# A chunked delta-rule scan in which batch 1 runs two steps behind batch 0 and w @ S is written one quarter on

## The chip, the cores and the metric

One core of a Trainium2 chip. The metric is the device time of one execution in microseconds (us), the median of the runs.

## The reference, cut to what matters

The model takes x of 2 x 1024 x 128 and applies three layers, each on a layer norm of x and added to x: a mixture of experts (top 1 of 8), an attention layer, and the same mixture of experts again. The change lies in the attention layer, in its delta rule, with 4 heads of 32 channels and chunks of 32 tokens, so 32 steps for each of the 2 batches:

```python
def step(S, inp):
    qi, ki, ui, wi = inp
    attn = jnp.tril(qi @ ki.transpose(0, 1, 3, 2))
    u_i = ui - wi @ S
    o_i = qi @ S + attn @ u_i
    return (S + ki.transpose(0, 1, 3, 2) @ u_i, o_i)
S0 = jnp.zeros((b, h, dk, dv), dtype=q.dtype)
S, o = jax.lax.scan(step, S0, (mov(q), mov(k), mov(u), mov(w)))
```

Each step needs the state S that the step before it left. The two batches have states of their own and don't depend on each other.

## The kernel before, in words

The program is a row of blocks that run one after the other: constants, `moe_ffn` (first), `attn_project`, `attn_delta`, `attn_mix`, `moe_ffn` (second). All data are fp32. Within a block each engine has its own program, written out in order, and semaphores join them.

`attn_delta` does in turn: the inverse of each chunk's triangular matrix (16 steps of products by `product`, L760, with masks by VectorE), scores and the u and w of all chunks (`scores`, `product`, `u0`), then the scan (299.56 to 362.05 us of the span), and last `intra`/`add_intra`, the products with u that need no state.

The scan is what the change touches. The state of a batch lies in `SB[:, b, :]`, 128 x 128, four heads as four blocks on the diagonal. For a step n and a batch b the chunk is quarter `c = n % 4` of tile `n // 4`. One step of one batch is a ring of four pieces:

- `w_state` (L886, TensorE): w @ S into partitions 32c to 32c+31 of bank b. The stationary operand is 128 rows x 32 columns, so the product uses all rows of the array and one quarter of its columns, the quarter in which its output lies. It waits for `s_ready`, the state after step n-1.
- `subtract` (L1090, VectorE): u = u - w @ S, on 32 partitions, from bank b into `U` (its tile has the name XN in the profile). It waits for `ws_psum`.
- `add_state` (L901, TensorE): k.T @ u, added into bank 2 + b. Its operands lie on 32 partitions (rows of quarter c), its output on all 128. It waits for `u_ready`.
- `state` (L1095, VectorE): the bank times a block mask, into `SB[:, b, :]` (d_SB). It waits for `s_psum`, and lets `w_state` of the next step go.

Beside the ring stands `q_state` (L893, TensorE): q @ S into the output bank (4 to 7), in quarter c too. It needs the state alone and nothing in the scan waits for it. In the profile every matmul of fp32 shows as two passes, each with its own weight load, so one product is x2, and the two products of both batches x4.

TensorE's program of one step is: w of batch 0, w of batch 1, q of batch 0, q of batch 1, add of batch 0, add of batch 1; in the first eight steps two transposes follow (`turn_fl`, L910, 128 x 128), which have nothing to do with the scan. VectorE's is: subtract 0, subtract 1, state 0, state 1; after steps 7, 15, 23 and 31 two reductions follow (`v_stats`, L1100 and L1101), which have nothing to do with the scan either. Both engines take their instructions in this order. All four w and q products of a step lie in the same column quarter c, and both adds on the same row quarter c.

Of the kernel before, what the change touches and what calls it, by code (L numbers as in the profile page):

```python
# [11 lines left out]
P = 128  # L12
# [664 lines left out]
def attn_delta(nc, cst, mem, banks, B, L, NH):  # L677
# [24 lines left out]
    with ExitStack() as ctx:  # L702
# [28 lines left out]
        m_psum, m_ready = sem("m_psum"), sem("m_ready")  # L731
        ws_psum = sem("ws_psum")
        u_ready = sem("u_ready")
        s_psum, s_ready = sem("s_psum"), sem("s_ready")
        oi_psum, oi_taken = sem("oi_psum"), sem("oi_taken")
# [20 lines left out]
        def product(pe, bank, lhs, slot):  # L756

            for t in range(TB):
                for a in range(NH):
                    mm = pe.matmul(bank[a * C:(a + 1) * C, t * P:(t + 1) * P], lhs(t, a), BD[:, slot, t * NH + a, :], start=True, stop=True)  # L760
            return mm

        def o_place(tile):
# [3 lines left out]
        with nc.Block() as block:  # L767

            @block.tensor
            def _(pe):  # L770
# [109 lines left out]
                def w_state(b, n):  # L880

                    c, t = n % CT, n // CT
                    cols = slice((b * TH + t) * P + c * C, (b * TH + t) * P + (c + 1) * C)
                    if n > 0:
                        pe.wait_ge(s_ready, n * B + b - B + 1)
                    pe.matmul(banks[b][c * C:(c + 1) * C, 0:P], WT[:, cols], SB[:, b, :], start=True, stop=True).then_inc(ws_psum, 1)  # L886

# [8 lines left out]
                def add_state(b, n):  # L896

                    c, t = n % CT, n // CT
                    rows, tile = slice(c * C, (c + 1) * C), b * TH + t
                    pe.wait_ge(u_ready, n * B + b + 1)  # L900
                    pe.matmul(banks[2 + b][:, 0:P], K[rows, tile, :], U[rows, tile, :], start=(n == 0),  # L901
                              stop=(n == STEPS_S - 1), skip_group_check=True).then_inc(s_psum, 1)

# [9 lines left out]

                for n in range(STEPS_S):
                    w_state(0, n)
                    w_state(1, n)
                    if n == STEPS_S // 2:

                        pe.wait_ge(fl_taken, NG)
                    q_state(0, n)  # L920
                    q_state(1, n)
                    add_state(0, n)
                    add_state(1, n)
                    if 2 * n < NT:
                        turn_fl(2 * n)
                        turn_fl(2 * n + 1)

                pe.wait_ge(u_ready, B * STEPS_S)
                pe.wait_ge(s_ready, B * STEPS_S)

# [96 lines left out]
            def _(ve):  # L1027
# [57 lines left out]
                def subtract(b, n):  # L1085

                    c, tile = n % CT, b * TH + n // CT
                    rows = slice(c * C, (c + 1) * C)
                    ve.wait_ge(ws_psum, n * B + b + 1)
                    ve.tensor_tensor(U[rows, tile, :], U[rows, tile, :], banks[b][rows, 0:P], ALU.subtract).then_inc(u_ready, 1)  # L1090

                def state(b, n):

                    ve.wait_ge(s_psum, n * B + b + 1)
                    ve.tensor_tensor(SB[:, b, :], banks[2 + b][:, 0:P], cst["blk"][:], ALU.mult).then_inc(s_ready, 1)  # L1095

# [5 lines left out]

                for n in range(STEPS_S):
                    subtract(0, n)
                    subtract(1, n)
                    state(0, n)
                    state(1, n)
                    if n % 8 == 7:
                        if n == 7:
                            ve.wait_ge(vsq_ready, 1)  # L1110
                        v_stats(n // 8)
# [702 lines left out]
```

## Time and profile before

| | us |
|---|---|
| median of 3 runs | 565.75 |
| the three runs | 565.56, 565.75, 574.91 |
| the profiled execution, its own time | 564.4 |
| its span | 562.6 |
| TensorE busy (share of the span) | 406.0 (72%) |
| VectorE busy (share) | 319.2 (57%) |
| granted TensorE clock, mean over the span | 0.867 |
| the scan, within the span | 299.56 to 362.05 |

The span is the time from the first to the last instruction in the profile; 1.8 us of the execution lie outside of it. PE is a matmul on TensorE, PEld its weight load, DVE is VectorE, ACT ScalarE. A clock of 1.00 is 2.4 GHz, of 0.50 is 1.2 GHz.

### The profile page before, as it was taken

Reading aid. Unit: us, or ns where it says so; the run is one execution under the profiler, and the core shown is the slowest. Engines: PE = TensorE matmul, PEld = TensorE weight load, DVE = VectorE, ACT = ScalarE, POOL = GpSimd, SP = SyncE. Lnnn points to the kernel's source line nnn. Section 1 sums busy time; section 2 is a strip of 40 time slices with the busy share of each in tenths; the row PEclk is TensorE's granted clock in tenths of the full one; section 3 lists DMA queues with packets and bytes.
Section 4 is the critical chain, followed back from the end, with each engine's and each line's share of the span. In section 5 each row is a group of like instructions: output and inputs, shape, how many; then the busy total and the mean of one; then the engine's idle time right before and its main releaser. Section 6 shows DMA issues by size and latency. Waiting matters only on the chain. (4 is left out here: it accounts for less than half of the span.)

```text
span 562.6 us, 12845 instructions
## 1 busy us (share of the span) xinstructions
PE 406.0 (72%) x5009; PEld 319.8 (57%) x5010; DVE 319.2 (57%) x819; ACT 225.3 (40%) x453; POOL 142.4 (25%) x154
## 2 busy tenths in 40 slices
PE   0776599925985668889999988977996370059990
PEld 0664399913545557767787666753454360059980
DVE  4550465436968498777455556455488846026533
ACT  1233055614556367877342000174566221015550
POOL 4427135520006792000000000020222202714441
PEclk9999899976899759999899999986998555569996
DMA  9963401130000000000000000047000082141005
GB/s 190 279 197 91 121 21 38 33 93 2 0 0 1 3 3 4 5 5 3 2 3 1 1 1 1 1 92 152 1 1 0 0 269 81 52 118 36 33 28 164
DMA packets 32709, 29.92 MB, mean 53 GB/s; under 512 B 6800, under 2 KB 25776, under 8 KB 32656
## 3 DMA queue, kind: packets, MB, share of 16 engines
q1 hardware_dynamic: 23760, 20.96, 13.3%
q10 hardware_dynamic: 6400, 3.08, 3.3%
q0 software_dynamic: 2496, 5.13, 2.8%
q8 instruction: 38, 0.62, 0.5%
q14 instruction: 15, 0.12, 0.1%
HBM read 16.54 MB, written 9.21 MB: 46 GB/s over the span
## 5 line engine op out<-in xcount | busy, mean ns | idle before, releaser
L303 ACT ACTIVATE hT<-bank,b1s 128x128 f32<-128x128 f32 x184 | 52.4, 370 | 92.2 <-PE bank L260 91.3
L206 POOL DMA_INDIRECT ysort<-Y,row x46 | 44.8, 974 | 71.3 <-DVE Y L382 65.2
L260 PE MATMUL bank<-xT,w1s 128*128 (+1 forms) x368 | 51.0, 283 | 3.5 <-DVE xT L405 3.5
L276 PE MATMUL bank<-W,hT 128*128 x368 | 50.4, 280 | 3.1 <-ACT hT L303 2.9
L260 PEld LDWEIGHTS bank<-xT,w1s 128*128 128x128 f32 x368 | 46.6, 198 | 4.7 <-DVE xT L405 4.1
L276 PEld LDWEIGHTS bank<-W,hT 128*128 128x128 f32 x368 | 44.6, 191 | 5.3 <-issue 4.8
L1382 POOL TENSOR_TENSOR m_DSQ<-DEL 128x512 f32<-128x512 f32 x4 | 4.1, 1041 | 159.2 <-POOLq L767 156.5
L1054 DVE TENSOR_TENSOR d_BD<-bank,quarter 128x2048 f32<-128x2048 f32 x16 | 36.5, 2288 | 13.5 <-PE bank L760 13.5
L199 POOL DMA_INDIRECT xsort<-xr,pos x32 | 31.4, 980 | 48.4 <-DVE pos L361 39.3
L964 ACT ACTIVATE d_BD<-d_TP 32x512 f32<-32x512 f32 x64 | 40.5, 633 | 0.9
L248 PE MATMUL bank<-ident,xs 128*128 128x128 f32 x46 | 8.3, 318 | 29.3 <-DMA xs<-xsort 29.3
L1095 DVE TENSOR_TENSOR d_SB<-bank,blk 128x128 f32<-128x128 f32 x64 | 16.5, 292 | 17.5 <-PE bank L901 17.5
L760 PE MATMUL bank<-d_BD,d_ATP 128*32 128x128 f32 x512 | 19.5, 293 | 6.4 <-ACT d_BD L964 6.4
L901 PE MATMUL bank<-XN,K 32*128 32x128 f32 x128 | 22.6, 296 | 1.4 <-DVE XN L1090 1.4
L886 PE MATMUL bank<-d_SB,KBT 128*32 128x128 f32 x128 | 20.1, 280 | 4.6 <-DVE d_SB L1095 3.7
L382 DVE TENSOR_TENSOR Y<-bank,b2t 128x128 f32 (+1 forms) x46 | 13.3, 288 | 17.8 <-PE bank L276 14.7
L248 PEld LDWEIGHTS bank<-ident,xs 128*128 128x128 f32 x46 | 6.4, 164 | 29.8 <-issue 29.5
L376 DVE COPY b1s<-b1T 128x4 f32 x46 | 9.2, 200 | 24.5 <-ACT hT L303 10.6
L1000 ACT ACTIVATE d_TMP<-bank 128x512 f32<-128x512 f32 x4 | 2.4, 598 | 48.3 <-PE bank L935 48.3
L1090 DVE TENSOR_TENSOR XN<-XN,bank 32x128 f32<-32x128 f32 x64 | 16.0, 283 | 9.2 <-PE bank L886 9.2
L901 PEld LDWEIGHTS bank<-XN,K 32*128 32x128 f32 x128 | 16.5, 185 | 8.0 <-DVE XN L1090 8.0
L378 DVE COPY w1s<-W 128x512 f32 x46 | 20.8, 453 | 0.0
(297 smaller groups left out, 928.7 us busy)
## 6 DMA issues: line engine op xcount, KB each, us to landing
W<-in_L_ffn_w SPq DMA_DIRECT2D x2, 2048.0 KB, 12.7
xsort<-pad ACTq DMA_DIRECT2D x2, 1483.5 KB, 20.4
xs<-xsort SPq DMA_DIRECT2D x10, 258.0 KB, 4.0
G<-ysort SPq DMA_DIRECT2D x8, 256.0 KB, 4.0
b2bc<-in_L_ffn_b SPq DMA_DIRECT2D x2, 512.0 KB, 19.6
m_pairs<-FS SPq DMA_DIRECT2D x4, 256.0 KB, 5.0
m_pairs<-firT SPq DMA_DIRECT2D x4, 256.0 KB, 4.9
m_pairs<-VP SPq DMA_DIRECT2D x4, 256.0 KB, 5.1
```

Of the source, the lines that this page charges most:

```text
L199: gp.indirect_dma_start(xsort, bass.IndirectOffsetOnAxis(pos[:, t:t + 1], 0), xr[:, t, :], None).then_inc(scattered, 16)
L206: gp.indirect_dma_start(ysort, bass.IndirectOffsetOnAxis(row[:, t:t + 1], 0), Y[:, t, :], None).then_inc(y_stored, 16)
L260: mm = pe.matmul(pH[s % 2][:, j * P:(j + 1) * P], w1s[:, s, j * P:(j + 1) * P], xT[:, bass.ds(t, 1), :], start=True, stop=True)
L276: mm = pe.matmul(pY[s % 2][:, 0:D], hT[:, s % 2, j, :], W2[:, bass.ds(e, 1), j, :], start=(j == 0), stop=(j == FC - 1))
L303: act.activation(hT[:, s % 2, j, :], pH[s % 2][:, j * P:(j + 1) * P], ACT.Gelu, bias=b1s[:, s, j:j + 1]).then_inc(h_ready, 1)
L378: ve.tensor_copy(w1s[:, s, :], W1[:, bass.ds(e, 1), :]).then_inc(w1_staged, 1)
L760: mm = pe.matmul(bank[a * C:(a + 1) * C, t * P:(t + 1) * P], lhs(t, a), BD[:, slot, t * NH + a, :], start=True, stop=True)
L886: pe.matmul(banks[b][c * C:(c + 1) * C, 0:P], WT[:, cols], SB[:, b, :], start=True, stop=True).then_inc(ws_psum, 1)
L901: pe.matmul(banks[2 + b][:, 0:P], K[rows, tile, :], U[rows, tile, :], start=(n == 0), stop=(n == STEPS_S - 1), skip_group_check=True).then ...
L964: cp = act.activation(spread_dst(i % 2, a), blocks(TP[a * C:(a + 1) * C, i % NG, :]), ACT.Copy)
L1054: ve.tensor_tensor(BD[:, 2 + i % 2, :, :].rearrange("p s (a n) -> p s a n", n=C), all_blocks(banks[i % 2][:]), mask, ALU.mult).then_inc(z_ ...
L1095: ve.tensor_tensor(SB[:, b, :], banks[2 + b][:, 0:P], cst["blk"][:], ALU.mult).then_inc(s_ready, 1)
```

## The change

Batch 1 runs two steps behind batch 0 (`LAG = 2`): the loops on TensorE and VectorE now have 34 iterations instead of 32, and iteration n does step n of batch 0 and step n - 2 of batch 1. Iterations 0 and 1 have batch 0 alone, iterations 32 and 33 batch 1 alone. The product w @ S of step n is written to column quarter (n + 1) % 4 of its bank (`w_rows`) and read there by `subtract`, whose other operands stay on quarter n % 4. So in iteration n the w products lie in quarters n+1 (batch 0) and n-1 (batch 1), the q products in quarters n and n-2, each modulo 4: four different ones. The adds lie on row quarters n and n-2. The four semaphores of the ring are kept per batch, each wait being for the same event as before. `turn_fl` stays in iterations 0 to 7, `v_stats` behind iterations 7, 15, 23 and 31.

```diff
--- before.py
+++ after.py
@@ -729,9 +729,7 @@
         ut_psum, ut_ready = sem("ut_psum"), sem("ut_ready")
         u0_psum, u0_ready = sem("u0_psum"), sem("u0_ready")
         m_psum, m_ready = sem("m_psum"), sem("m_ready")
-        ws_psum = sem("ws_psum")
-        u_ready = sem("u_ready")
-        s_psum, s_ready = sem("s_psum"), sem("s_ready")
+        ws_psum, u_ready, s_psum, s_ready = ([sem(f"{n}{b}") for b in range(B)] for n in ("ws_psum", "u_ready", "s_psum", "s_ready"))
         oi_psum, oi_taken = sem("oi_psum"), sem("oi_taken")
         o_psum = sem("o_psum")
         short_fir = sem("short_fir")
@@ -759,6 +757,17 @@
                 for a in range(NH):
                     mm = pe.matmul(bank[a * C:(a + 1) * C, t * P:(t + 1) * P], lhs(t, a), BD[:, slot, t * NH + a, :], start=True, stop=True)
             return mm
+
+        LAG = 2
+
+        def w_rows(b, n):
+
+            c = (n + 1) % CT
+            return slice(c * C, (c + 1) * C)
+
+        def active(b, n):
+
+            return 0 <= n - b * LAG < STEPS_S
 
         def o_place(tile):
 
@@ -882,8 +891,8 @@
                     c, t = n % CT, n // CT
                     cols = slice((b * TH + t) * P + c * C, (b * TH + t) * P + (c + 1) * C)
                     if n > 0:
-                        pe.wait_ge(s_ready, n * B + b - B + 1)
-                    pe.matmul(banks[b][c * C:(c + 1) * C, 0:P], WT[:, cols], SB[:, b, :], start=True, stop=True).then_inc(ws_psum, 1)
+                        pe.wait_ge(s_ready[b], n)
+                    pe.matmul(banks[b][w_rows(b, n), 0:P], WT[:, cols], SB[:, b, :], start=True, stop=True).then_inc(ws_psum[b], 1)
 
                 def q_state(b, n):
 
@@ -897,9 +906,9 @@
 
                     c, t = n % CT, n // CT
                     rows, tile = slice(c * C, (c + 1) * C), b * TH + t
-                    pe.wait_ge(u_ready, n * B + b + 1)
+                    pe.wait_ge(u_ready[b], n + 1)
                     pe.matmul(banks[2 + b][:, 0:P], K[rows, tile, :], U[rows, tile, :], start=(n == 0),
-                              stop=(n == STEPS_S - 1), skip_group_check=True).then_inc(s_psum, 1)
+                              stop=(n == STEPS_S - 1), skip_group_check=True).then_inc(s_psum[b], 1)
 
 
                 def turn_fl(n):
@@ -911,22 +920,24 @@
                     if t == TB - 1:
                         tr.then_inc(fl_psum, 1)
 
-                for n in range(STEPS_S):
-                    w_state(0, n)
-                    w_state(1, n)
+                for n in range(STEPS_S + LAG):
+                    both = [b for b in range(B) if active(b, n)]
+                    for b in both:
+                        w_state(b, n - b * LAG)
                     if n == STEPS_S // 2:
 
                         pe.wait_ge(fl_taken, NG)
-                    q_state(0, n)
-                    q_state(1, n)
-                    add_state(0, n)
-                    add_state(1, n)
+                    for b in both:
+                        q_state(b, n - b * LAG)
+                    for b in both:
+                        add_state(b, n - b * LAG)
                     if 2 * n < NT:
                         turn_fl(2 * n)
                         turn_fl(2 * n + 1)
 
-                pe.wait_ge(u_ready, B * STEPS_S)
-                pe.wait_ge(s_ready, B * STEPS_S)
+                for b in range(B):
+                    pe.wait_ge(u_ready[b], STEPS_S)
+                    pe.wait_ge(s_ready[b], STEPS_S)
 
                 def intra(g):
 
@@ -1086,13 +1097,13 @@
 
                     c, tile = n % CT, b * TH + n // CT
                     rows = slice(c * C, (c + 1) * C)
-                    ve.wait_ge(ws_psum, n * B + b + 1)
-                    ve.tensor_tensor(U[rows, tile, :], U[rows, tile, :], banks[b][rows, 0:P], ALU.subtract).then_inc(u_ready, 1)
+                    ve.wait_ge(ws_psum[b], n + 1)
+                    ve.tensor_tensor(U[rows, tile, :], U[rows, tile, :], banks[b][w_rows(b, n), 0:P], ALU.subtract).then_inc(u_ready[b], 1)
 
                 def state(b, n):
 
-                    ve.wait_ge(s_psum, n * B + b + 1)
-                    ve.tensor_tensor(SB[:, b, :], banks[2 + b][:, 0:P], cst["blk"][:], ALU.mult).then_inc(s_ready, 1)
+                    ve.wait_ge(s_psum[b], n + 1)
+                    ve.tensor_tensor(SB[:, b, :], banks[2 + b][:, 0:P], cst["blk"][:], ALU.mult).then_inc(s_ready[b], 1)
 
                 def v_stats(c):
 
@@ -1100,12 +1111,13 @@
                     ve.tensor_reduce(mem["ST"][:, part, 1, 3, :], V[:, part, :].rearrange("p t (h d) -> p t h d", h=NH), AX.X, ALU.max)
                     ve.tensor_reduce(mem["ms"][:, part, 3, :], VSQ[:, part, :].rearrange("p t (h d) -> p t h d", h=NH), AX.X, ALU.add)
 
-                for n in range(STEPS_S):
-                    subtract(0, n)
-                    subtract(1, n)
-                    state(0, n)
-                    state(1, n)
-                    if n % 8 == 7:
+                for n in range(STEPS_S + LAG):
+                    both = [b for b in range(B) if active(b, n)]
+                    for b in both:
+                        subtract(b, n - b * LAG)
+                    for b in both:
+                        state(b, n - b * LAG)
+                    if n % 8 == 7 and n < STEPS_S:
                         if n == 7:
                             ve.wait_ge(vsq_ready, 1)
                         v_stats(n // 8)
```

TensorE at the end of the scan. Banks 0 and 1 take w @ S of batch 0 and 1, banks 5 and 7 q @ S, banks 2 and 3 the state; L935 is `intra`, the stage behind the scan. Before:

```order
L886 MATMUL bank0<-d_SB,KBT 32x128
L886 MATMUL bank1<-d_SB,KBT 32x128
L893 MATMUL bank5<-d_SB,QT 32x128
L893 MATMUL bank7<-d_SB,QT 32x128
L901 MATMUL bank2<-XN,K 128x128
L901 MATMUL bank3<-XN,K 128x128
L935 MATMUL bank0<-d_BD,XN 32x128 x16
```

The same place after the change (w is L895, q L902, add L910, `intra` L946):

```order
L895 MATMUL bank0<-d_SB,KBT 32x128
L895 MATMUL bank1<-d_SB,KBT 32x128
L902 MATMUL bank5<-d_SB,QT 32x128
L902 MATMUL bank7<-d_SB,QT 32x128
L910 MATMUL bank2<-XN,K 128x128
L910 MATMUL bank3<-XN,K 128x128
L895 MATMUL bank1<-d_SB,KBT 32x128
L902 MATMUL bank7<-d_SB,QT 32x128
L910 MATMUL bank3<-XN,K 128x128
L895 MATMUL bank1<-d_SB,KBT 32x128
L902 MATMUL bank7<-d_SB,QT 32x128
L910 MATMUL bank3<-XN,K 128x128
```

The order within an iteration is as it was; what has moved is that two iterations with batch 1 alone stand ahead of `intra` (and two with batch 0 alone at the start of the scan).

VectorE at the same place; L1100 and L1101 are the reductions of `v_stats`, banks as above. Before:

```order
L1090 TENSOR_TENSOR XN<-XN,bank0 32x128
L1090 TENSOR_TENSOR XN<-XN,bank1 32x128
L1095 TENSOR_TENSOR d_SB<-bank2,blk 128x128
L1095 TENSOR_TENSOR d_SB<-bank3,blk 128x128
L1100 TENSOR_REDUCE ST<-V 128x4x4
L1101 TENSOR_REDUCE ms<-d_BD 128x4x4
```

After (subtract is L1101, state L1106, the reductions L1111 and L1112):

```order
L1101 TENSOR_TENSOR XN<-XN,bank0 32x128
L1101 TENSOR_TENSOR XN<-XN,bank1 32x128
L1106 TENSOR_TENSOR d_SB<-bank2,blk 128x128
L1106 TENSOR_TENSOR d_SB<-bank3,blk 128x128
L1111 TENSOR_REDUCE ST<-V 128x4x4
L1112 TENSOR_REDUCE ms<-d_BD 128x4x4
L1101 TENSOR_TENSOR XN<-XN,bank1 32x128
L1106 TENSOR_TENSOR d_SB<-bank3,blk 128x128
L1101 TENSOR_TENSOR XN<-XN,bank1 32x128
L1106 TENSOR_TENSOR d_SB<-bank3,blk 128x128
```

The last pair of reductions, which was the end of VectorE's part of the scan, now stands ahead of the last two steps of batch 1.

## Rows read from the trace of the kernel before

**Rows 1.** Who waited for whom in the scan: total us, times, longest us

```profile
DVE d_SB L1095 <- PE bank L901: 17.5, 32, 0.6
...
PEld bank L886 <- DVE d_SB L1095: 9.4, 31, 0.4
DVE XN L1090 <- PE bank L886: 9.2, 29, 0.6
PEld bank L901 <- DVE XN L1090: 8.0, 32, 0.8
```

**Rows 2.** The scan: length, busy PE, PEld, DVE, ACT, POOL, TensorE's clock, DMA

```profile
299.60:362.05 62.45, 56.99 (x400) 41.59 (x400) 35.85 (x135) 2.98 (x5) 0.00 (x0) 1.00 0.00 1
```

**Rows 3.** Timeline of one ordinary step: start, us, engine, line; idle before it

```profile
333.34 0.36 PEld L886 LDWEIGHTS bank<-d_SB,KBT 128*32 128x32 f32 x4 [0.35 <-DVE d_SB L1095]
333.78 0.50 DVE L1090 TENSOR_TENSOR XN<-XN,bank 32x128 f32<-32x128 f32 x2 [0.27 <-PE bank L886]
333.81 0.60 PE L893 MATMUL bank<-d_SB,QT 128*32 128x128 f32 x4
334.33 0.52 PEld L901 LDWEIGHTS bank<-XN,K 32*128 32x128 f32 x4 [0.20 <-DVE XN L1090]
334.86 0.52 DVE L1095 TENSOR_TENSOR d_SB<-bank,blk 128x128 f32<-128x128 f32 x2 [0.57 <-PE bank L901]
335.20 0.36 PEld L886 LDWEIGHTS bank<-d_SB,KBT 128*32 128x32 f32 x4 [0.35 <-DVE d_SB L1095]
```

**Rows 4.** Single products, passes or VectorE instructions, from narrower windows

```profile
329.82 0.27 PE L893 MATMUL bank<-d_SB,QT 128*32 128x128 f32 x1
...
333.34 0.41 PE L886 MATMUL bank<-d_SB,KBT 128*32 128x128 f32 x2 [0.16 <-DVE d_SB L1095]
...
334.01 0.28 DVE L1090 TENSOR_TENSOR XN<-XN,bank 32x128 f32<-32x128 f32 x1
...
334.34 0.48 PE L901 MATMUL bank<-XN,K 32*128 32x128 f32 x2
...
334.86 0.29 DVE L1095 TENSOR_TENSOR d_SB<-bank,blk 128x128 f32<-128x128 f32 x1 [0.57 <-PE bank L901]
```

**Rows 5.** Timeline of a step with the two transposes

```profile
312.53 0.71 PE L901 MATMUL bank<-XN,K 32*128 32x128 f32 x4
...
313.16 0.20 PEld L910 LDWEIGHTS bank<-ident,FLt 128*128 128x128 f32 x2
...
313.53 0.36 PEld L886 LDWEIGHTS bank<-d_SB,KBT 128*32 128x32 f32 x4 [0.17 <-DVE d_SB L1095]
...
315.53 0.36 PEld L886 LDWEIGHTS bank<-d_SB,KBT 128*32 128x32 f32 x4 [0.17 <-DVE d_SB L1095]
```

**Rows 6.** Timeline of a step behind the two reductions of VectorE

```profile
330.54 0.52 DVE L1095 TENSOR_TENSOR d_SB<-bank,blk 128x128 f32<-128x128 f32 x2 [0.56 <-PE bank L901]
...
330.97 0.68 DVE L1100 TENSOR_REDUCE ST<-V 128x16 f32<-128x512 f32 x1
...
331.56 0.68 DVE L1101 TENSOR_REDUCE ms<-d_BD 128x16 f32<-128x512 f32 x1
332.16 0.46 DVE L1090 TENSOR_TENSOR XN<-XN,bank 32x128 f32<-32x128 f32 x2
```

**Rows 7.** Timeline behind the scan: 16 products of L935, four quarters in turn

```profile
365.16 1.08 PE L935 MATMUL bank<-d_ATP,XN 128*32 128x128 f32 x32
```

**Rows 8.** Busy us by stretch, as rows 2: before and behind the scan

```profile
276.82:280.20 3.38, 3.15 (x41) 2.75 (x33) 1.32 (x3) 2.83 (x5) 0.00 (x0) 1.00 0.00 0
280.23:283.60 3.37, 3.37 (x41) 2.71 (x43) 1.32 (x2) 0.00 (x0) 0.00 (x0) 0.50 0.00 0
...
372.40:375.79 3.39, 1.31 (x8) 0.84 (x8) 3.28 (x7) 1.90 (x5) 1.87 (x2) 1.00 0.51 117
375.80:379.20 3.40, 2.44 (x10) 1.44 (x11) 3.40 (x6) 3.31 (x7) 1.04 (x1) 0.50 0.98 205
```

**Rows 9.** Timeline before the scan, at half clock: 16 products of `product`, four quarters in turn

```profile
273.64 1.93 PE L760 MATMUL bank<-d_BD,VB 128*32 128x128 f32 x32
```

## The prediction

> **What bounds the kernel now.** I read the waits of the scan first, then the scan as one stretch, then one step in narrow windows. In the waits the reader is to see a ring: VectorE waits for TensorE 32 times ahead of the state (17.5 us in all) and 29 times ahead of the subtract (9.2), and TensorE's weight loads wait for VectorE ahead of w (9.4) and of the add (8.0) [rows 1]. No other engine and no DMA is in it; ScalarE is busy 2.98 us of 62.45, and TensorE has its full clock throughout [rows 2].
>
> The narrow windows tell which wait is real. In the ordinary step the w products start at 333.34 and those of the next step at 335.20, so a step takes 1.86 us [rows 3]. Batch 0's ring alone is shorter. The second w pass ends 0.41 after the start of the first [rows 4] and the subtract starts at 333.78, +0.44 [rows 3]; it takes 0.28 [rows 4] and ends at 334.06. The add starts only at 334.33 [rows 3]. The profile puts this wait down to VectorE, but batch 0's subtract had been done for 0.27. Between a VectorE end and the weight load it releases there are otherwise only 0.05 (the state of batch 0 starts at 334.86, takes 0.29, and w loads at 335.20 [rows 3, 4]), so the add could load at 334.11. What holds it is TensorE's own order: the four q passes stand ahead of it, start 0.11 apart from 333.81 (four in 0.60 [rows 3], one takes 0.27 [rows 4]), the last at 334.14, and the load of another shape comes 0.19 to 0.20 behind it [rows 3]. These four passes and the four of w all lie in one column quarter. The two add passes take 0.48 to their end (0.49 from the load), the state starts 0.04 later, takes 0.29 [rows 4], and the release 0.05.
>
> **The change part by part.**
>
> *Quarters.* Of products in four quarters by turns there is a row: 32 passes of L935, the same shape as w and q, take 1.08 us, so (1.08 - 0.27) / 31 = 0.026 per pass against 0.11 in one quarter [rows 7]. With w of batch 1 and both q in three other quarters, the q passes need not queue behind w. Batch 1's state ends 0.22 to 0.29 after batch 0's, so its w loads at about +0.29, the q passes start right behind it, and the last starts at about +0.29 + 0.02 + 0.11 + 0.03 = +0.45; with 0.20 for the change of shape the add could load at +0.65. Batch 0's subtract lets it go at +0.44 + 0.28 + 0.05 = +0.77. So q is off the path, with 0.12 to spare, and the ring sets the step: 0.44 + 0.28 + 0.05 + 0.49 + 0.04 + 0.29 + 0.05 = 1.64 us. An ordinary step saves 0.22. What is late next is VectorE and the latency of each piece, not TensorE's order.
>
> *Batch 1 in the ring.* Its pieces follow batch 0's. Now the second subtract starts 0.22 after the first [rows 3, 4]. No row shows two subtracts on different quarters, so its place is bounded: +0.22 as now, or, with nothing laid over the first and a gap of 0.05, +0.33. I take 0.28, the end of the first. Batch 1's add then loads at 0.77 + 0.28 + 0.01 = +1.06 and ends at +1.55, its state +1.59 to +1.88, its w at +1.93: the offset stays 0.29, the step stays 1.64. The two adds lie on different row quarters and need not queue either; even if they did batch 0's last pass starts at +0.99 and batch 1's first at +1.06, so nothing changes. Reading bank b one quarter off the output costs nothing as an operation added; the nearest durations are 0.28 for the 32-partition subtract and 0.29 for the 128-partition state [rows 4], so the bound is 0 to 0.01 x 34 = 0.3 us, and no reason makes it a gain. I take 0.
>
> By the Trainium skill, VectorE: DVE Perf Modes, section "Two Vector instructions with no wait between them", an instruction that starts on another quadrant than the one before is held until that one has finished. No run here shows it yet; by it the second subtract comes at +0.28 and the result is the one taken above, without it the sum would be 0.4 us lower.
>
> *Steps with transposes.* Before they take 2.00 (313.53 to 315.53 [rows 5]): the transposes load 0.19 after the last add pass starts (312.53 + 0.71 - 0.27 = 312.97), and w 0.37 after that, 0.14 later than its state allows. After: batch 1's last add pass starts at 1.06 + 0.215 = +1.28 (two passes end 0.49 from the load, the last takes 0.27), the transposes load at +1.47, w at +1.84. Iterations 2 to 7 take 1.84; by the two bounds of the second subtract 1.78 or 1.89, so 6 x 0.06 = 0.4 us either way. In iterations 0 and 1 batch 1 is absent, the transposes load at +0.99 + 0.19 = +1.18 and are over at +1.55: hidden, 1.64.
>
> *The reductions.* The first starts 0.20 after batch 1's state starts (330.54 + 0.23 = 330.77, then 330.97), and the subtract comes 1.19 later, 1.39 after that state's start [rows 6]. Before, w behind them starts at 330.54 + 0.29 + 0.05 = 330.88 and the next at 333.34 [rows 3]: a step of 2.46, so 0.60 more than 1.86, three times, while the fourth pair lies behind the scan. In the shorter ring there is less slack: the subtract is due 0.50 after batch 1's state starts (1.64 + 0.44 - 1.59), so it is 0.89 late, behind iterations 15 and 23; 0.69 behind iteration 7, whose w is 0.20 late anyway; and behind iteration 31, where batch 1 alone goes on (due at 0.29 + 0.05 + 0.44 = 0.78), 0.61. Sum 3.1 us. They now start as early as they do now; if the subtract had to await the end of the second reduction (332.24 instead of 332.16), 4 x 0.08 = 0.3 more.
>
> *Lag.* 34 iterations instead of 32, the added two at 1.64. They stand ahead of the stage behind the scan, which needs the last u of batch 1, and nothing hides them: 3.3 us, in the sum below.
>
> *Sum.* 28 x 1.64 + 6 x 1.84 + 3.1 = 45.9 + 11.0 + 3.1 = 60.0 us. Before: 8 x 2.00 + 24 x 1.86 + about 1.6 = 62.2; the trace has 62.49 (299.56 to 362.05). The gain is 62.5 - 60.0 = 2.5. No DMA is issued in the scan and no queue is passed. Taken from the profiled execution's 564.4 that is 562.0; the median of the runs is 1.35 above that execution, so I forecast 563.4.
>
> **The rivals.**
>
> *The clock falls in the scan: slower than before.* The granted clock never fell in the scan, where TensorE was busy 57.0 of 62.45 us [rows 2]. But busy time does not guard it: it was 0.50 in the stretch from 280.23, behind one busy for 3.15 of 3.38 us, and in the stretch from 375.80, behind one busy for 1.31 of 3.39 with eight matmuls [rows 8]. After the change the same products lie upon each other and then pause, longest at the reductions, and at the scan's end batch 1 is alone. At half clock 32 passes take 1.93 instead of 1.08 [rows 7, 9], a pass round 0.11 more; with two rounds and a longer last pass in w and again in the add I estimate 0.5 to 0.6 per step, 2.2 instead of 1.64. So a stretch of 3.4 us at half clock holds 1.5 steps for 2.1 and loses 0.9. It decides once more than about three such stretches fall, which eats the 2.5. If the clock falls at each of the four reductions and once behind the scan (up to 1.5 there), the loss is 5.1 and the time 568.5; if every other stretch of the scan is cold, some nine, it is 8 and the time about 571. Against it speaks that the number of passes per us rises.
>
> *The quarters don't overlap.* Then the q passes follow w of batch 1: they start at +0.52, the last at +0.85, the add loads at +1.05 instead of +0.77, and an ordinary iteration takes 1.92, one with transposes about 2.05. 4 x 1.64 + 6 x 2.05 + 24 x 1.92 + about 2.3 for the reductions = 67.2, 4.7 more than before: 570.5. The row of L935 speaks against it [rows 7]: by it neighbours in other quarters do overlap. The Trainium skill, TensorE: Matmul & The Clock Gate, section "Part 3: Packing small matmuls — row/col tiling", says that "LDWEIGHTS overlaps with in-flight MATMULs only when row_grp differs"; all four products here use all rows, so by that rule this rival would hold. The trace disagrees with it, with 0.026 us per pass.
>
> *The lag and the reductions eat all.* If only the ordinary steps gained and the transposed ones did not (6 x 0.16), with the reductions 0.3 dearer, the gain is 1.2: 564.6. That is inside the forecast's own spread.
>
> **How the numbers follow.** Forecast, ring of 1.64 with the clock held or down once: 0.63. Clock falls repeatedly: 0.26. No overlap: 0.07. Gain larger than 4.5, by a reason that I don't see: 0.04. The forecast's own range is 561.5 to 565.5: the bounds above give 0.4 + 0.3 + 0.3, and a single clock stretch falling elsewhere behind the scan, since all later work starts 2.5 us sooner, some 1.5. The range reaches into the clock rival: 560.8 to 570.0. 2% are 11.3 us, about what a measurement of this kernel can tell from no change; no case of mine gains that, and only a scan cold for most of its length (34 x 0.55 = 19 us) loses it. So faster 0.01, same 0.94, slower 0.05.
>
> **What would show it.** Right: w starts 1.64 apart in ordinary iterations and 1.84 with transposes; the add loads 0.05 behind its own subtract; the q passes start within 0.2 of w of batch 1; the scan lasts 60 us from first w to last state. Wrong: a granted clock under 1.00 in the scan; q passes 0.11 apart behind w of batch 1; a second subtract much later than 0.33 behind the first; a subtract longer than 0.29.

## The result and the profile after

| | before | after |
|---|---|---|
| median of 4 runs each, us | 570.33 | 583.05 |
| all runs | 565.56, 565.75, 574.91, 579.55 | 582.10, 582.83, 583.27, 583.49 |
| ratio, 95% interval | | 1.029 [1.026, 1.033] |
| span of the profiled execution | 562.6 | 580.5 |
| ahead of the scan | 299.6 | 302.1 |
| the scan | 62.5 | 79.0 |
| behind the scan | 200.5 | 199.4 |
| mean granted clock over the span | 0.867 | 0.789 |

The change makes the kernel slower, and the scan alone is 16.5 of the 17.9 us by which the span grew. The ratio leaves out executions that fell in a slower state, so it is not 583.05 / 570.33 = 1.022. Further runs of the unchanged kernel, reported below, spread from 566.8 to 589.5 us, so what is firm of the loss is the part that the profile shows in the scan. The page's clock row (40 slices, here of 14.5 us each) shows where to look:

```profile
PE 424.5 (73%) x5009; PEld 323.6 (56%) x5010; DVE 322.2 (56%) x819; ACT 225.7 (39%) x453; POOL 142.2 (24%) x154
...
PEclk9999799958797679999775555566899555559996
```

Slices 22 to 26 (counted from 1) lie wholly in the scan, and stand at 5, half clock. TensorE's busy time went up by 18.5 us with the same number of matmuls, 12.1 of it in the scan (69.06 against 56.99), where the same matmuls take longer. The busy rows by stretch (length, busy PE, PEld, DVE, ACT, POOL, clock, DMA), first the whole scan as in [rows 2], then its two parts, then a stretch behind it that is at full clock again:

```profile
302.08:381.08 79.00, 69.06 (x400) 38.94 (x400) 41.59 (x136) 2.39 (x4) 0.00 (x0) 0.52 0.00 1
...
301.50:304.80 3.30, 1.91 (x14) 1.01 (x14) 1.38 (x4) 0.49 (x1) 0.00 (x0) 1.00 0.00 0
304.95:381.00 76.05, 67.00 (x387) 37.86 (x386) 40.65 (x133) 2.39 (x4) 0.00 (x0) 0.50 0.00 1
387.00:397.00 10.00, 7.35 (x104) 5.96 (x96) 3.73 (x6) 6.43 (x11) 3.03 (x3) 1.00 0.14 34
```

The scan starts at full clock (2.4 GHz), loses it 2.8 us later, in iteration 1, with batch 0 alone in the ring, and runs at 1.2 GHz to its end. Only the dense stage behind it brings the clock back, at 386.8 (from 381.2 to 386.7 TensorE was busy for 5.47 of 5.50 us). In the 3.30 us ahead of the fall TensorE was busy for 1.91 us with 14 passes. The first 3.30 us of the scan in the kernel before, to be held against that:

```profile
299.60:302.90 3.30, 3.30 (x25) 2.61 (x26) 1.49 (x6) 0.59 (x1) 0.00 (x0) 1.00 0.00 0
```

The waits show the same ring as [rows 1], with the wait ahead of the add now on top:

```profile
PEld bank L910 <- DVE XN L1101: 22.5, 34, 1.3
DVE d_SB L1106 <- PE bank L910: 19.9, 34, 0.9
...
DVE XN L1101 <- PE bank L895: 15.7, 30, 0.9
PEld bank L895 <- DVE d_SB L1106: 10.6, 30, 0.7
```

TensorE's load for the add waits for VectorE 22.5 us instead of 8.0: the q passes no longer stand in its way, it really waits for the subtract (and at half clock most pieces of the ring take longer). One iteration at half clock, to be held against the step of [rows 3] (w is L895, q L902, subtract L1101, add L910, state L1106):

```profile
342.40 0.45 PEld L895 LDWEIGHTS bank<-d_SB,KBT 128*32 128x32 f32 x3 [0.36 <-DVE d_SB L1106]
...
342.73 0.43 PE L902 MATMUL bank<-d_SB,QT 128*32 128x128 f32 x2
...
342.95 0.43 PE L902 MATMUL bank<-d_SB,QT 128*32 128x128 f32 x2
343.08 0.60 DVE L1101 TENSOR_TENSOR XN<-XN,bank 32x128 f32<-32x128 f32 x2 [0.41 <-PE bank L895]
343.42 0.81 PEld L910 LDWEIGHTS bank<-XN,K 32*128 32x128 f32 x4 [0.50 <-DVE XN L1101]
...
344.25 0.61 DVE L1106 TENSOR_TENSOR d_SB<-bank,blk 128x128 f32<-128x128 f32 x2 [0.57 <-PE bank L910]
344.59 0.44 PEld L895 LDWEIGHTS bank<-d_SB,KBT 128*32 128x32 f32 x3 [0.36 <-DVE d_SB L1106]
```

From 342.40 to 344.59 are 2.19 us against 1.86 at full clock before. The order of things is the one aimed at: the four q passes start in two pairs, at 342.73 and 342.95, right behind w of batch 1, and the add loads 0.06 behind the end of its own subtract (343.08 + 0.28). At full clock one iteration was to be seen whole in this run, the first, with batch 0 alone and its two transposes:

```profile
302.08 0.11 PEld L895 LDWEIGHTS bank<-d_SB,KBT 128*32 128x32 f32 x1 [1.19 <-DVE XN L1072]
...
302.59 0.28 DVE L1101 TENSOR_TENSOR XN<-XN,bank 32x128 f32<-32x128 f32 x1 [0.57 <-PE bank L895]
302.92 0.29 PEld L910 LDWEIGHTS bank<-XN,K 32*128 32x128 f32 x2 [0.70 <-DVE XN L1101]
...
303.79 0.11 PEld L895 LDWEIGHTS bank<-d_SB,KBT 128*32 128x32 f32 x1 [0.25 <-DVE d_SB L1106]
```

That is 1.71 us, with the subtract 0.51 behind w instead of the 0.44 of [rows 3].

Not all iterations take 2.19. The six with both batches and transposes take 2.67 each (w at 305.65 and, six later, at 321.64), and the ones behind the second and third pair of reductions 2.97 (339.43 to 342.40):

```profile
305.65 0.14 PEld L895 LDWEIGHTS bank<-d_SB,KBT 128*32 128x32 f32 x2 [0.33 <-DVE d_SB L1106]
...
321.64 0.13 PEld L895 LDWEIGHTS bank<-d_SB,KBT 128*32 128x32 f32 x2 [0.33 <-issue]
...
339.43 0.45 PEld L895 LDWEIGHTS bank<-d_SB,KBT 128*32 128x32 f32 x3 [0.36 <-DVE d_SB L1106]
...
340.21 0.68 DVE L1112 TENSOR_REDUCE ms<-d_BD 128x16 f32<-128x512 f32 x1
340.90 0.60 DVE L1101 TENSOR_TENSOR XN<-XN,bank 32x128 f32<-32x128 f32 x2
```

### The profile page after: what moved, and what is told of

Same layout as the page of the kernel before. It is cut to its first block and busy times, and to the rows that moved or that the text cites. A ratio compares the mean times of both kernels' runs of the same rounds, so it can differ in the third digit from the quotient of the medians.

```text
span 580.5 us, 12846 instructions
## 1 busy us (share of the span) xinstructions
PE 424.5 (73%) x5009; PEld 323.6 (56%) x5010; DVE 322.2 (56%) x819; ACT 225.7 (39%) x453; POOL 142.2 (24%) x154
## 5 line engine op out<-in xcount | busy, mean ns | idle before, releaser
L910 PE MATMUL bank<-XN,K 32*128 32x128 f32 x128 | 35.9, 491 | 7.4 <-DVE XN L1101 6.5
L910 PEld LDWEIGHTS bank<-XN,K 32*128 32x128 f32 x128 | 26.0, 302 | 22.5 <-DVE XN L1101 22.5
L895 PE MATMUL bank<-d_SB,KBT 128*32 128x128 f32 x128 | 28.6, 417 | 3.0 <-DVE XN L1072 0.8
L248 PE MATMUL bank<-ident,xs 128*128 128x128 f32 x46 | 8.8, 328 | 29.3 <-DMA xs<-xsort 29.3
L1106 DVE TENSOR_TENSOR d_SB<-bank,blk 128x128 f32<-128x128 f32 x64 | 18.7, 292 | 20.7 <-PE bank L910 19.9
L1101 DVE TENSOR_TENSOR XN<-XN,bank 32x128 f32<-32x128 f32 x64 | 18.2, 284 | 16.8 <-PE bank L895 15.7
L248 PEld LDWEIGHTS bank<-ident,xs 128*128 128x128 f32 x46 | 6.7, 170 | 30.0 <-issue 29.6
L902 PE MATMUL bank<-d_SB,QT 128*32 128x128 f32 x128 | 21.3, 417 | 0.0
## 6 DMA issues: line engine op xcount, KB each, us to landing
W<-in_L_ffn_w SPq DMA_DIRECT2D x2, 2048.0 KB, 12.1
```

The lines of the kernel that those rows point to most:

```text
L248: tr = pe.transpose(pX[c % 2][:, t * P:(t + 1) * P], xs[:, g + t, 0:D], ident[:])
L895: pe.matmul(banks[b][w_rows(b, n), 0:P], WT[:, cols], SB[:, b, :], start=True, stop=True).then_inc(ws_psum[b], 1)
L902: pe.matmul(o_place(tile)[c * C:(c + 1) * C, :], QT[:, cols], SB[:, b, :], start=(tile % TB == 0), stop=True, skip_group_check=True)
```

## The experiments

The runs were made in several jobs on different chips, each with runs of the kernel before beside it, and times of different jobs are not to be compared (the unchanged kernel's ran from 565.6 to 589.5 us). What is compared is therefore the scan within each profile: its length from first w to last state, its clock, and the time from one w to the next. The clock was looked at in one profiled execution of each run. The rest of the span can't be held against the change: without the run behind a pause, the scans start at 299.6 to 312.4 us, and what follows them takes 199 to 203. A table comes first, the runs one by one behind it.

Four theories of the lost clock go through the expectations: A, TensorE has too little to do in each step; B, the lag is to blame; C, only passes that lie upon each other in several quarters lose the clock; D, the thin entrance loses it, and a scan of this kind stays at the clock with which it enters. An ordinary iteration is one without transposes and not behind reductions.

| run | scan, us | clock in it | ordinary iteration, us | whole run, us (before in the same job) |
|---|---|---|---|---|
| before | 62.5 | 1.00 | 1.86 | 565.56 to 579.55 |
| the change | 79.0 | 0.52 | 2.18 | 583.05 (570.33) |
| lag alone | 82.8 | 0.51 | 2.37 | 590.62 (573.22) |
| quarters alone | 84.9 | 0.51 | 2.60 | 591.18 (573.22) |
| change + one product | 68.3 | 0.85 | 1.65 to 1.76 | 576.69 (573.22) |
| change + two products | 65.6 | 1.00 | 1.85 | 576.20 (573.22) |
| before without q | 68.6 | 0.63 | 1.65, then 2.19 | 581.87 (586.44) |
| before behind a pause | 101.8 | 0.50 | 3.02 | 620.52 (586.44) |
| change + products at the start | 73.8 | 0.62 | 2.18 after the start | 585.53 (586.44) |
| change + products tuned | 72.5 | 0.73 | 1.65 to 1.75, then 2.38 | 584.33 (586.44) |
| before again | 62.5 | 1.00 | 1.86 | 580.15 (571.74) |
| change + two products again | 65.6 | 1.00 | 1.85 | 584.42 (571.74) |
| before + products | 62.8 | 1.00 | 1.86 | 571.82 (571.74) |
| tuned + 32-row products | 62.5 | 1.00 | 1.66 to 1.76 | 564.78 (581.03) |

**The two halves of the change.** Lag alone:

```diff
-            c = (n + 1) % CT
+            c = n % CT
```

> The change without its quarters: batch 1 two steps behind, w @ S in quarter n as before. Then w and q of one batch share a quarter, and the passes lie two by two upon each other instead of four. Theory A (the clock falls because the w and q passes lie upon each other, so that TensorE's array is at work for less of each step): less overlap than in the change, so a clock above the change's; if it holds, a step of 1.70 and 565 us, if it falls nonetheless, 2.2 to 2.3 per step and 583. Theory B (the lag alone is to blame: adds on two row quarters, thin first iterations): the clock falls as in the change, 583 us.

Quarters alone:

```diff
-        LAG = 2
+        LAG = 0
```

> The change without its lag: 32 iterations with both batches at the same step, w @ S one quarter on. Both w in one quarter, both q in the next. Theory A: overlap two by two as in the run with the lag alone, and the same fate as that run (clock held: 1.65 to 1.7 per step, 557 to 560 us; fallen: 2.2 per step, 578). Theory B: the clock holds, since nothing is staggered, 557 to 560 us.

Both lose the clock. The scan of the lag alone, then of the quarters alone:

```profile
305.36:388.15 82.79, 74.71 (x400) 47.13 (x400) 39.29 (x136) 2.57 (x5) 0.00 (x0) 0.51 0.00 1
```

```profile
301.36:386.25 84.89, 83.30 (x400) 52.98 (x400) 40.02 (x135) 2.56 (x5) 0.00 (x0) 0.51 0.00 1
```

So theory B falls: with nothing staggered the clock goes too. Theory A had said that both share one fate, and they do; its other guess for the lag alone, a clock above the change's, was wrong. Each half takes q passes off TensorE's order by laying them on w passes, and either is enough. In a kernel at half clock the two still add up in the way intended (quarters alone 2.60, lag alone 2.37, both 2.18; before 3.02, by a run below): the less stands in TensorE's order, the shorter the step. TensorE is busy 83.3 of 84.9 us in the second row, and has half the clock: the busy column says nothing on whether the clock is held.

**More work in the scan.** Products of constants were added to the change between the q products and the adds, in the quarter of the last q product so that they follow it; nobody reads them. With one:

```diff
+        FILL = lambda n: 4 if n % 8 == 0 and n > 0 else 1
...
+                    for k in range(FILL(n)):
+                        q4 = slice((n + 2) % CT * C, ((n + 2) % CT + 1) * C)
+                        pe.matmul(banks[2][q4, P:2 * P], cst["ones"][:, 0:C], cst["blk"][:], start=False, stop=True, skip_group_check=True)
                     for b in both:
                         add_state(b, n - b * LAG)
```

> The change, with one product of constants more per iteration (128 rows x 32 columns, two passes, in the quarter of the last q product so that it follows it), four in the iterations behind the reductions, where TensorE waits; its results are read by nobody. Theory A: TensorE works longer in each iteration and the clock holds or returns; if it does, 1.74 per step and 564 to 566 us. Theory B: the clock stays at half, and each step is longer than the change's by up to 0.2, 583 to 590 us.

With two, the number is `4 if n % 8 == 0 and n > 0 else 2`:

> As the run with one product more, with two per iteration. Theory A: if one does not hold the clock, two do; 1.96 per step at full clock, 570 to 573 us. Theory B: half clock, 590 us or more.

Rows of the run with one product, by stretch, and a row of its timeline at the point where the clock came back:

```profile
305.50:307.00 1.50, 1.07 (x10) 0.58 (x10) 0.47 (x2) 0.57 (x1) 0.00 (x0) 1.00 0.00 0
307.20:327.40 20.20, 19.84 (x121) 12.45 (x122) 9.24 (x30) 2.39 (x4) 0.00 (x0) 0.50 0.00 1
327.60:373.70 46.10, 41.39 (x362) 27.87 (x360) 30.85 (x104) 0.00 (x0) 0.00 (x0) 1.00 0.01 1
```

```profile
325.96 1.81 PE L935 MATMUL bank<-blk,ones 128*32 128x128 f32 x8
...
328.57 0.31 PEld L896 LDWEIGHTS bank<-d_SB,KBT 128*32 128x32 f32 x3 [0.57 <-DVE d_SB L1110]
...
330.22 0.14 PEld L896 LDWEIGHTS bank<-d_SB,KBT 128*32 128x32 f32 x2 [0.26 <-DVE d_SB L1110]
```

It lost the clock at the start like the change, and had it back behind the eight added passes of iteration 8, to the end. The next w starts are 1.65 and 1.74 apart, and go on so by turns; in the longer ones the add waits for the added product. So with a product more the ring of the change takes at full clock 1.65 where the product is not in its way, about what was predicted without it (1.64). With two products the whole scan ran at full clock:

```profile
306.82:372.37 65.55, 57.32 (x552) 40.87 (x552) 39.28 (x136) 3.02 (x5) 0.00 (x0) 1.00 0.01 1
```

More work makes the scan 13.4 us shorter than the change's. That fits theory A, and no theory in which the work itself is the cost. But at 1.85 per iteration the gain of the ring has gone into the products, and the two iterations of the lag remain: 3 us more than before.

**Less work without any overlap.** The kernel before, with `q_state` in steps 0 and 16 alone; its output lacks the other q @ S terms:

```diff
-                    q_state(0, n)
-                    q_state(1, n)
+                    if n % (STEPS_S // 2) == 0:
+                        q_state(0, n)
+                        q_state(1, n)
```

> The kernel before, which has no overlap of w and q passes, no lag and no quarters, without the product q @ S in 30 of its 32 steps (its output lacks these terms). Theory A as it now stands (what counts is for how long TensorE works in each step, whatever the way in which that gets less): the clock falls in the scan, 2.1 to 2.4 per step, scan 75 us or more. Theory C (only passes that lie upon each other in several quarters make the clock fall): the clock holds, 1.65 per step, scan about 56 us.

```profile
309.10:327.10 18.00, 15.75 (x100) 10.55 (x100) 10.70 (x40) 2.96 (x5) 0.00 (x0) 1.00 0.00 1
327.30:377.60 50.30, 49.09 (x181) 29.18 (x180) 27.72 (x95) 0.00 (x0) 0.00 (x0) 0.50 0.00 0
```

The clock held for the eight steps with transposes and two behind them, then fell for good. It fell later than expected, so the scan is 68.6 and not 75. That is still 12 us more than the 56 of theory C, which also wanted the clock held, so C is out: overlap in several quarters is not needed. The one ordinary step that lies at full clock but for its last 0.3 us took 1.65, so the ring of before without q in its way is as long as predicted for the change. Taking 30 steps' q products away makes the scan 6.1 us longer.

**Entering the scan at half clock.** The kernel before, with 17 copies of VectorE on a scratch tile, for which TensorE waits ahead of the scan:

```diff
+                for _ in range(16):
+                    cp = ve.tensor_copy(TMP[:, 0, :], TMP[:, 1, :])
+                    ch.step(cp)
+                ve.tensor_copy(TMP[:, 0, :], TMP[:, 1, :]).then_inc(paused, 1)
...
+                pe.wait_ge(paused, 1)
```

> The kernel before with a pause of TensorE ahead of the scan (17 copies of VectorE, some 6 to 12 us), so that it enters the scan at half clock. Theory A: its scan works long enough in each step to get the clock back within a few steps; scan at most 5 us over the 62.5 of before. Theory D (the clock of the changed kernel fell at the entrance of its scan and any scan of this kind stays where it enters): the clock stays at half to the end of the scan, 80 us or more.

```profile
314.88:416.63 101.75, 101.40 (x400) 67.68 (x400) 39.88 (x135) 2.39 (x4) 0.00 (x0) 0.50 0.00 1
```

```profile
314.88 0.61 PEld L888 LDWEIGHTS bank<-d_SB,KBT 128*32 128x32 f32 x4 [9.09 <-issue]
```

After 9.1 us of idle time TensorE enters at half clock and stays there for all 32 steps, at 3.61 each with transposes and 3.02 without. Here theory A was wrong, and D right in this part: the scan of before, too, doesn't win the clock back. In the profiles at hand it only keeps one that it has when it comes.

**The start alone.** The change with `FILL = lambda n: 3 if n < 2 else 2 if n < 8 else 0`:

> The change with products more in its first eight iterations alone (three in iterations 0 and 1, two in 2 to 7), none later. Theory A: full clock in the first eight iterations, it falls behind them, at the latest at the first pair of reductions, and doesn't return: 24 iterations near 2.18, scan about 75 us. Theory D (only the thin entrance tips it): full clock throughout, 1.64 per step, scan 61 us. It also shows what an ordinary iteration takes at full clock without products added: 1.64 predicted.

```profile
306.65:324.40 17.75, 16.60 (x156) 11.61 (x156) 10.30 (x35) 3.03 (x5) 0.00 (x0) 1.00 0.00 1
324.60:380.40 55.80, 49.59 (x280) 28.29 (x280) 30.73 (x101) 0.00 (x0) 0.00 (x0) 0.50 0.00 1
```

```profile
321.29 0.19 PEld L896 LDWEIGHTS bank<-d_SB,KBT 128*32 128x32 f32 x3 [0.17 <-DVE d_SB L1110]
...
321.83 0.67 DVE L1116 TENSOR_REDUCE ms<-d_BD 128x16 f32<-128x512 f32 x1
322.52 0.60 DVE L1105 TENSOR_TENSOR XN<-XN,bank 32x128 f32<-32x128 f32 x2
322.85 0.62 PEld L911 LDWEIGHTS bank<-XN,K 32*128 32x128 f32 x4 [1.33 <-DVE XN L1105]
...
323.72 0.14 PEld L896 LDWEIGHTS bank<-d_SB,KBT 128*32 128x32 f32 x2 [0.25 <-DVE d_SB L1110]
```

Full clock as long as there are products, and lost behind the first pair of reductions, in the second iteration after the last of them. So a thin entrance is enough to lose the clock, and a full one doesn't save it. What loses it then is not told apart: the fall comes 1.6 us behind a wait of 1.33 us for the reductions, and no run shows an ordinary iteration of the change without products at full clock from its start to its end. This run was meant to time one and didn't.

**Products where TensorE waits.** The change with `FILL = lambda n: 3 if n < 2 or n in (8, 16, 24) else 2 if n < 8 else 1`:

> The change with products more where TensorE waits: three in iterations 0, 1, 8, 16 and 24, two in 2 to 7, one elsewhere. Theory A: full clock throughout, 1.66 to 1.75 per ordinary iteration as in the run with one product more, scan 62 to 64 us, so level with the kernel before within 0.5%. Theory D asks for the entrance alone and expects the same clock.

```profile
307.00:340.20 33.20, 31.33 (x284) 21.84 (x284) 20.95 (x71) 2.39 (x4) 0.00 (x0) 1.00 0.01 2
340.40:379.40 39.00, 33.98 (x216) 21.47 (x216) 18.35 (x65) 0.00 (x0) 0.00 (x0) 0.50 0.00 0
```

The full clock was expected throughout. It was held for 33 us, then lost behind the second pair of reductions, and the six added passes at the third did not bring it back. The run with one product more, with eight added passes behind each pair, kept it behind the second and the third. One product is at the edge.

**The clock ahead of the scan.** In the change the full clock had been back for only 0.5 us when the scan began, in the kernel before for 16. Two runs speak against this as the cause. With one product more the clock had been full for 15 us when the scan began and fell all the same, and in the kernel before plus products, which comes below, it was back for 1.5 us only and stayed. The stretches ahead of the scan of the change, ahead of that with one product more, and ahead of and in that of before plus products:

```profile
297.00:301.40 4.40, 4.29 (x56) 3.36 (x47) 1.45 (x3) 1.91 (x2) 0.00 (x0) 0.50 0.00 0
```

```profile
290.20:305.40 15.20, 13.77 (x229) 11.81 (x220) 9.21 (x14) 7.49 (x12) 0.00 (x0) 1.00 0.01 2
```

```profile
299.80:306.00 6.20, 6.20 (x80) 5.36 (x80) 2.08 (x3) 0.55 (x1) 0.00 (x0) 0.50 0.00 0
306.40:370.60 64.20, 59.30 (x423) 43.84 (x421) 37.13 (x137) 3.97 (x5) 0.00 (x0) 1.00 0.00 1
```

**The spread of the kernel before.** In three jobs it had taken 565.6 to 579.6, 573.2 and 586.4 us. It was run again unchanged, together with the change plus two products, and with itself plus three products in steps 8, 16 and 24:

```diff
+                    for k in range(3 if n in (8, 16, 24) else 0):
+                        pe.matmul(banks[2][n % CT * C:(n % CT + 1) * C, P:2 * P], cst["ones"][:, 0:C], cst["blk"][:], start=False, stop=True, skip_group_check=True)
                     add_state(0, n)
```

> The kernel before, unchanged, to see its own spread: in some jobs it took 565.6, in others 573 to 586. If its scan too can lose the clock part of the way and not get it back (a step at half clock costs 3.02 instead of 1.86, so 1.16 for each step that is left), its times lie anywhere from 565 up to 565.6 + 32 x 1.16 = 603, and the mean clock of each execution falls as its time rises. If the spread has another source, the clock is the same in all.

> The change with two products more per iteration and four behind the reductions again, in rounds. Theory A: every execution holds the clock, all within 0.5% of each other, 568 to 577 us with a scan of 65.5; slower than the kernel before only where that one holds its clock to the end.

> The kernel before with three products of constants more (six passes) in steps 8, 16 and 24, where TensorE waits 0.8 us for the reductions. If the clock of the kernel before is lost at the reductions, this holds it: 565 to 567 us in every execution, faster than the kernel before in its median. If it is lost elsewhere, the spread stays.

The scans were 62.48, 65.55 and 62.80 us, all at full clock. The profiled execution of the unchanged kernel had a span of 575.4 with that scan at its full clock:

```profile
312.42:374.90 62.48, 57.05 (x400) 41.62 (x400) 35.85 (x135) 3.02 (x5) 0.00 (x0) 1.00 0.00 1
```

Its scan starts at 312.4 instead of 299.6, and the first transposes of the sorted rows (L248) at 74.0 instead of 64.4: most of those 13 us arise in the first 74 us of the program, long ahead of anything that was changed. Of its 4 runs here, two (572.0 and 577.3) had mean clocks of 0.852 and 0.864 and two (583.0 and 589.5) 0.831 and 0.830. The same job has 14 more runs of the same kernel: twelve took 566.8 to 574.2 us at mean clocks of 0.848 to 0.865, and two 586.8 and 587.1 at 0.829 and 0.834. So there is spread that doesn't come from the clock, some 10 us among the runs at 0.848 and more, and a longer group, from 583 us up, at a lower clock. An estimate from these rows: 0.03 of clock less over 585 us is 35 us at half clock, or 12 steps of 3.02, and 12 x 1.16 = 14 us more, which is about the distance between the groups. So the long ones may have lost the clock late in the scan; it isn't shown, since their clock by stretch wasn't recorded. The added products in before made no difference: ratio 0.999 [0.994, 1.003]. The expectation that they steady it fell, 566.0 to 576.8 us in 10 runs, though none of these is in the longer group. The change plus two products was expected within 0.5% of itself at 568 to 577 us; its 4 runs took 577.2 to 593.7 at mean clocks of 0.862 to 0.830, so that expectation fell too, and that every execution holds the clock isn't shown. It is 1.021 [1.015, 1.028] against before, so whether it is 2% slower is unclear; its scan explains 3 us, or 0.5%, and the rest stays open.

**Work on a quarter of the rows.** The tuned kernel above with one product of 32 rows more in every iteration from 8 on, of the shape of the adds, so without a change of shape:

```diff
+                    if n >= 8:
+                        pe.matmul(banks[0][:, P:2 * P], cst["ones"][0:C, :], cst["blk"][0:C, :], start=False, stop=True, skip_group_check=True)
```

> The kernel of the run with the products more where TensorE waits (which lost the clock at iteration 15), with one product of 32 rows x 128 columns more behind the adds of every iteration from 8 on, where it costs about 0.05 us. If work on a quarter of the rows helps to hold the clock, it is held throughout: 1.70 to 1.80 per iteration, scan 63 to 65 us. If such work counts for little, the clock is lost as without it, 2.4 per step behind that point.

```profile
300.65:363.17 62.52, 57.45 (x552) 40.17 (x552) 40.70 (x136) 3.02 (x5) 0.00 (x0) 1.00 0.01 1
```

```profile
339.23 0.34 PEld L896 LDWEIGHTS bank<-d_SB,KBT 128*32 128x32 f32 x3 [0.33 <-DVE d_SB L1112]
...
340.90 0.14 PEld L896 LDWEIGHTS bank<-d_SB,KBT 128*32 128x32 f32 x2 [0.27 <-DVE d_SB L1112]
```

Full clock throughout, 1.67 and 1.74 by turns in ordinary iterations, and a scan of 62.52 us, level with before. As one run against one run that lost the clock at the edge, it doesn't prove that the 32-row product did it. Its 564.78 us is no more than the lower end of what the unchanged kernel reaches, and its scan gives no reason for a gain. No version was shown to beat the kernel before.

## Why the prediction was wrong, point by point

The forecast of 563.4 (560.8 to 570.0) was wrong, and of its signs of being wrong the first came true, a granted clock under 1.00 in the scan. Its sum was near the mark as far as the ring at full clock goes. The step that failed is the one that put 1.64 on every iteration at a clock that is held: it was 0.50 from iteration 1 to the end, and the scan took 79.0 us instead of 60.0.

- **Quarters.** Right. The q passes left the path, the add waits for its own subtract. The rival "the quarters don't overlap" fell. The rule of the Trainium skill cited with it (TensorE: Matmul & The Clock Gate, section "Part 3: Packing small matmuls — row/col tiling") is not what this trace shows for column quarters: the passes in different quarters start 0.02 behind each other though all use all rows.
- **The step of 1.64.** Borne out near it at full clock, though no ordinary iteration of the change itself was seen there: 1.71 in its first iteration with batch 0 alone, 1.65 in a step of before without q, 1.65 to 1.76 in the change with one product more. At half clock the estimate was 2.2 and 2.18 was measured.
- **Batch 1 in the ring.** The second subtract comes 0.32 behind the first (two in 0.60, one of 0.28), at the upper bound of 0.33, where 0.28 was taken. The offset of batch 1 is 0.32 instead of 0.29 and the step is as long. In an ordinary iteration this spacing says little, since batch 1's own w ends just then; the 0.22 of [rows 3], too, are the end of its w. The test is behind the reductions, where both w products are long done: there two subtracts on different quarters start 0.31 apart, behind the end of the first (340.90, two in 0.60; lag alone 0.30), and two on one quarter 0.19, ahead of its end ([rows 6], two in 0.46; quarters alone 0.21). This agrees with the rule of the Trainium skill, VectorE: DVE Perf Modes, section "Two Vector instructions with no wait between them".
- **Steps with transposes.** 1.84 was predicted; at full clock they took 1.88, with two products more. In the change, at half clock, they took 2.67.
- **The reductions.** 0.69 was predicted for the first pair. In the run with products at the start iteration 8 took 2.43 at full clock (321.29 to 323.72), 0.79 more than 1.64. Most of the difference was in the text as a bound: before, the subtract starts 0.08 ahead of the end of the second reduction [rows 6], in the change behind it (321.83 + 0.67 = 322.50, then 322.52). At half clock the second and third pair cost 2.97 - 2.18 = 0.79 each.
- **The sum.** This is where it failed. It put 1.64 on every iteration because the clock had been 1.00 throughout the scan before, and gave 0.26 to the rival that it falls. The clock fell in iteration 1. Of the 19.0 us that the scan took over the predicted 60.0, the 20 ordinary iterations at 2.18 or 2.19 make 10.9 and the six with transposes 5.0; the rest lies in the first two, behind the reductions and at the end.
- **The clock rival** had the place and the price per iteration right and two things wrong. It let the clock come back in every other stretch, hence "about 571", when the scan at half clock never gets it back, neither in the change nor in the kernel before behind a pause. And it held against itself that the number of passes per us rises. Where the clock was lost the number had fallen, 14 passes in 3.30 us (the first 0.6 us of them ahead of the scan) against 25 in before, since batch 0 is alone there. It can't be the number alone either, since the quarters alone, with both batches from the start, lose the clock as well. That TensorE's array is at work for less of each step when passes lie upon each other is what theory A says; no row measures that, so it is a reading of the runs and not shown. The case of a scan cold for its length stood in the text with 19 us, and outside the range.
- **What bounds the kernel.** "TensorE's own order" was taken for a pure cost of 0.22 us per step. The experiments without q and with products added show that the same work also kept the clock up: it cost 0.22 and saved what half the clock costs. A step of before is 1.86 with it, and 2.19 without q at half clock.

Still open is which measure of TensorE's work decides on the clock, by how much the scan of before is clear of the edge, and what spreads its runs over some 20 us.

## What to carry to other kernels

A wait that is TensorE's own queue of matmuls may be what keeps its clock up. Before matmuls are laid upon each other or taken away in a stretch that is bound by latency, put beside the gain what the stretch costs at half clock, for its whole length, because a latency-bound loop that has lost the clock may not get it back. When two executions are compared, look at the granted clock of the stretch first and at the busy share last: here it was 98% at half clock in one run and 87% at full clock in another.

## What was not expected of the hardware

- The clock has a memory in such a loop. An ordinary step of the same 32 takes 1.86 us when they are entered at full clock and 3.02 when entered at half clock, for 62.5 or 101.8 us in all, with no return in between.
- Removing work made the scan slower (62.5 to 68.6 us without q in 30 steps), and adding work made it faster (79.0 to 65.6 us with two products more per iteration).
- Two subtracts whose inputs are long ready start 0.31 us apart on different quarters, behind the end of the first, and 0.19 on one quarter, ahead of it.
- Passes in different quarters don't start in the order of the program: in the change's first iteration the first pass of q starts with the first of w at 302.08, ahead of w's second at 302.21.
